# Idle columns on TensorE around and inside the products of decay and V, in a cross-attention and expert kernel

## The chip, the cores and the metric

The kernel runs on one core of one Trainium2 chip. The metric is the device time of the kernel in microseconds (us), as the median of its runs. Beside it stands one profiled execution, with the span from its first to its last instruction, the times of each engine, and the clock that TensorE was granted.

The engines are called by their short names: PE (TensorE, matrix products; PEld is its weight load), DVE (VectorE), ACT (ScalarE), POOL (GpSimd) and SP (which issues DMAs).

## The reference

Two layers, each added to its input x, of 32 batches of 128 tokens with 256 features:

```python
# attention of the mLSTM kind: q = layernorm(x), k = v = ctx, 8 heads of 32 features
cs = cumsum(log_sigmoid(fg))
log_D = cs_s - cs_t + ig_t            # masked to t <= s
D = exp(log_D - max_t log_D)
C = (q k^T / sqrt(32)) * D
h = C / (max(|sum_t C|, exp(-max_log_D)) + 1e-6) @ v
x = x + groupnorm(h) * out_w
# mixture of 8 experts, two for each token
x = x + sum_k gate_k * (gelu(xn @ w1[e_k] + b1[e_k]) @ w2[e_k] + b2[e_k])
```

## The kernel before

The work has two parts. The first runs over eight steps of four batches each (SB = 4, j = 0 to 3): normalise x, turn x and ctx, gates, decay matrix, scores, the product with V, normalise h, add to x, route the tokens and scatter them to a table sorted by expert. The second part runs the experts over tiles of up to 256 rows from that table, and adds the results to the output.

In the first part each engine runs a list of helpers in an order that is written out by hand, and semaphores tie the engines together. One pass of `body(last, step, nxt, after)` holds pieces of four steps: the routing of `last`, the end of the attention of `step`, the decay matrix and first scores of `nxt`, and the turning and gates of `after`. So one period of the loop holds the work of one whole step, spread over four.

The names that matter for the change, on PE:

- `decay_args` (L942, L946, L949) builds the exponents of the decay matrix of one batch and half of its heads in one PSUM bank, `turn_bank`; ACT takes the exp of it (L706). Its last product is the identity times `never`, 512 columns in bf16.
- `scores(j)` (L997) makes the 24 products of q and k of one batch, in f16 halves of 32 rows. DVE multiplies the scores by the decay matrix (`c_of`, L1355) and counts up `s_cm`. The scores of the next batch wait for that count, since there is one place for scores.
- `times_v(j)` (L1011) makes 16 products of 128 rows and 33 columns in f32, eight heads by two: the weights are the 128x128 blocks of the product of scores and decay, and the columns are V with a column of ones. All go to the first 264 columns of one bank, `ps_h` (named `pv` in the profile). It waits for `s_vc` (V ready), `s_cm`, and `s_hev`: ACT's eviction of that bank for the batch before it (`h_out`, L726 and L727).
- `turn_a` (L977) turns a column of gates, on which the running maximum and the split of it (`running_max`, L1304, and `split`, L1322) wait on DVE. `turn_max` (L983) turns the running maximum.
- `gates` (L963), `log_f_sum` (L971), `turn`, `q_left`, `turn_xf`, `xf_left`, `logits` and `ranks` are the other work of PE in a period.

On DVE a period is a fixed list: the four `c_of`, `next_stats` and `next_norm`, `weights_low` (expert weights split into halves), `running_max` and `split`, `h_norm` (which waits for the last eviction of times-V, L1365), `h_scaled` (which waits for ACT's guess of the root, L638), `choose`, `x1_of`, `x1_stats` and `records`.

Batches 0 and 1 of a step's times-V run at the end of one pass and batches 2 and 3 at the start of the next. After the eighth step the same helpers are written out once more, with the first expert tiles laid between them.

Of the kernel before, what the change touches and what calls it, by code (L numbers as in the profile page):

```python
# [13 lines left out]
P = 128  # L14
# [32 lines left out]
def build(nc, x, ctx_in, igate_w, igate_b, fgate_w, fgate_b, out_w, gate_w, w1, b1, w2, b2, out):  # L47
# [5 lines left out]
    NE, _, F = w1.shape  # L53
    FC = F // P
    SB = 4
# [41 lines left out]
    with ExitStack() as ctx:  # L97
        def sb(name, shape, dt=F32):
            return ctx.enter_context(nc.sbuf_tensor(name, shape, dt))

        def sem(name):
            return ctx.enter_context(nc.semaphore(name))
# [24 lines left out]
        ident_h = sb("ident_bf16", [P, P], BF16)  # L127
        minus_h = sb("minus_ident_f16", [P, P], F16)
        never = sb("minus_big_above", [P, P], BF16)
# [97 lines left out]
        ps_h = ctx.enter_context(nc.psum_tensor("pv", [P, 512], F32))  # L227
# [77 lines left out]
        s_hev = sem("h_in_sbuf")  # L305
# [23 lines left out]
        def number(step):  # L329
            return step[0] * 2 + step[1]  # L330

        def some(step, n):

            return not (isinstance(step[0], int) and number(step) < n)
# [72 lines left out]
        with nc.Block() as block:  # L407
# [494 lines left out]
            def _(pe):  # L902
# [31 lines left out]
                def decay_args(step, j, r):  # L934

                    g = number(step)
                    if j == 0 and r == 0:
                        pe.wait_ge(s_sp, g * 2 + 2)
                    if j + r or some(step, 1):
                        pe.wait_ge(s_ee, g * (2 * SB) + (2 * j + r))  # L940
                    first = j * NH + r * HG
                    pe.matmul(ps_t[:, :], parts[:, step[1], 0, :],  # L942
                              pick[:, first:first + HG].unsqueeze(2).broadcast_to([3 * G, HG, P]),
                              start=True, stop=False)
                    for u in range(HG):
                        pe.matmul(ps_t[:, u * P:(u + 1) * P],  # L946
                                  unpick[:, first + u:first + u + 1].broadcast_to([3 * G, P]),
                                  parts[:, step[1], 1, :], start=False, stop=False)
                    pe.matmul(ps_t[:, :], ident_h[:, :], never[:, :].unsqueeze(1).broadcast_to([P, HG, P]),  # L949
                              start=False, stop=True).then_inc(s_ar, 1)  # L950
# [23 lines left out]
                def turn_a(step):  # L974
                    g = number(step)
                    pe.wait_ge(s_a, g + 1)
                    pe.transpose(ps_aT, acol[:, :, :].rearrange("p r g -> p (r g)"), ident[:, :]).then_inc(s_aT, 1)  # L977

                def turn_max(step):
                    g = number(step)  # L980
                    pe.wait_ge(s_run, g + 1)
                    pe.sem_inc(s_held, 1)
                    pe.transpose(ps_ab, runs[2 * G:, 1, :], ident[2 * G:3 * G, 2 * G:3 * G]).then_inc(s_ab, 1)  # L983

                def scores(step, j):

                    g = number(step)
                    if j == 0:
                        turned = 1 if isinstance(g, int) and g == NSTEP - 1 else 2
                        pe.wait_ge(s_ql, g * SB + turned * SB)  # L990
                    if j or some(step, 1):
                        pe.wait_ge(s_cm, g * SB + j)
                    for u in range(KC):
                        for n, (a, b) in enumerate(HALVES):
                            for k in range(HG):
                                r = slice(DH * k, DH * k + DH)
                                ins = pe.matmul(ps_s[:, k, u * P:(u + 1) * P], qkT[r, step[1], j, a, KC + u, :],  # L997
                                                qkT[r, step[1], j, b, u, :], start=(n == 0), stop=(n == 2))
                    ins.then_inc(s_s, 1)

                def times_v(step, j):
                    g = number(step)
                    if j == 0:
                        pe.wait_ge(s_vc, g + 1)
                    pe.wait_ge(s_cm, g * SB + j + 1)
                    if j or some(step, 1):
                        pe.wait_ge(s_hev, g * SB + j)
                    for u in range(KC):
                        for k in range(HG):
                            h = u * HG + k  # L1010
                            ins = pe.matmul(ps_h[:, h * (DH + 1):(h + 1) * (DH + 1)], E[:, j, k * KC + u, :],  # L1011
                                            vaug[:, step[1], j, h, :], start=True, stop=True)
                    ins.then_inc(s_pv, 1)

                def turn_xf(step, r):
                    g = number(step)
                    pe.wait_ge(s_xf, g * SB + 2 * r + 2)
                    if r:
                        pe.wait_ge(s_xl, g * (SB // 2) + r)
                    elif some(step, 1):  # L1020
                        pe.wait_ge(s_rec, g)
                    else:
                        pe.wait_ge(s_cd, 1)
                    for j in range(2):
                        for c in range(KC):
                            ins = pe.matmul(ps_x[:, (j * KC + c) * P:(j * KC + c + 1) * P],
                                            xfn[:, step[1], 2 * r + j, c * P:(c + 1) * P], ident[:, :],
                                            is_transpose=True, start=(j == 0 and c == 0), stop=(j == 1 and c == KC - 1))
                    ins.then_inc(s_xt, 1)
# [32 lines left out]
                def body(last, step, nxt, after):  # L1062
                    if step is not None:
                        scores(step, 3)
                        times_v(step, 2)
                    if nxt is not None:
                        turn_a(nxt)
                    if last is not None:
                        turn_xf(last, 0)
                    if step is not None:  # L1070
                        times_v(step, 3)
                    if nxt is not None:
                        decay_args(nxt, 0, 0)
                    if after is not None:
                        turn(after, 0)
                    if last is not None:
                        xf_left(last, 0)
                    if after is not None:
                        turn(after, 1)
                    if nxt is not None:  # L1080
                        decay_args(nxt, 0, 1)
                    if last is not None:
                        turn_xf(last, 1)
                    if after is not None:
                        q_left(after, 0)
                    if nxt is not None:
                        decay_args(nxt, 1, 0)
                    if last is not None:
                        xf_left(last, 1)
                    if after is not None:  # L1090
                        turn(after, 2)
                        q_left(after, 1)
                    if last is not None:
                        logits(last)
                    if after is not None:
                        turn(after, 3)
                    if nxt is not None:
                        decay_args(nxt, 1, 1)
                    if after is not None:
                        q_left(after, 2)  # L1100
                    if nxt is not None:
                        turn_max(nxt)
                    if after is not None:
                        q_left(after, 3)
                    if nxt is not None:
                        decay_args(nxt, 2, 0)
                        scores(nxt, 0)
                    if after is not None:
                        gates(after)
                    if nxt is not None:  # L1110
                        decay_args(nxt, 2, 1)
                        scores(nxt, 1)
                        times_v(nxt, 0)
                    if last is not None:
                        ranks(last)
                    if nxt is not None:
                        decay_args(nxt, 3, 0)
                        scores(nxt, 2)
                        times_v(nxt, 1)
                    if after is not None:  # L1120
                        log_f_sum(after)
                    if nxt is not None:
                        decay_args(nxt, 3, 1)
# [651 lines left out]
```

## Time and profile before

| | |
|---|---|
| median of 3 runs | 737.8 us (736.86 to 738.75) |
| the profiled execution, its own time | 738.3 us |
| its span | 736.5 us |
| mean granted clock of TensorE over the span | 0.884 |
| PE busy | 671.3 us (91%) |
| DVE busy | 529.6 us (72%) |
| ACT busy | 316.8 us (43%) |
| POOL busy | 196.2 us (27%) |

The granted clock is given as a share of full speed: 1.00 is 2.4 GHz and 0.50 is 1.2 GHz, and a value between them is the mean over a stretch with both. A wait in the profile is idle time of an engine, named after the instruction that ended it. Products on PE are pipelined, so the time from the start of one group to the start of the next is what a group costs, not its length in the row.

### The profile page before, as it was taken

What the parts mean: (1) busy time and instruction counts of PE and PEld (TensorE: products, weight loads), DVE (VectorE), ACT (ScalarE), POOL (GpSimd) and SP (SyncE); (2) the same over time, 40 slices, a digit from 0 to 9 for tenths busy, and PEclk for the clock granted to TensorE, in tenths of its full rate; (3) what the DMA queues carried; (4) which work ended last, traced back from release to release, by engine and by line L of the source; (5) the groups of instructions that cost most, each with busy time, mean ns of one, the idle gap of its engine ahead of it and who ended that gap; (6) DMA issues with size and microseconds to landing.
All of it is one profiled execution on the core that took longest, in us unless ns stands there. A gap on an engine that the chain in (4) does not pass through costs nothing. (4 is left out here: it accounts for less than half of the span.)

```text
span 736.5 us, 19825 instructions
## 1 busy us (share of the span) xinstructions
PE 671.3 (91%) x6379; PEld 568.2 (77%) x6380; DVE 529.6 (72%) x1434; ACT 316.8 (43%) x743; POOL 196.2 (27%) x178
## 2 busy tenths in 40 slices
PE   2397999898999899989999999999999999999994
PEld 1265868585868567878998998888988898898873
DVE  3659888989798958498778867657766666766652
ACT  4377575766575733345423323323323323323321
POOL 2000004140404032225335413313323322322334
PEclk9998785858575955699999999999999999999998
DMA  3534353645445121614336423223223223323000
GB/s 126 171 116 136 123 170 101 210 132 171 146 145 174 63 87 60 207 40 105 56 69 201 84 53 62 40 52 59 41 42 58 40 48 59 49 39 60 7 4 2
DMA packets 56037, 66.45 MB, mean 90 GB/s; under 512 B 6480, under 2 KB 51728, under 8 KB 55840
## 3 DMA queue, kind: packets, MB, share of 16 engines
q1 hardware_dynamic: 41552, 48.13, 21.3%
q0 software_dynamic: 14304, 17.32, 12.9%
q8 instruction: 43, 0.70, 0.4%
q14 instruction: 26, 0.21, 0.1%
q10 hardware_dynamic: 112, 0.08, 0.1%
HBM read 41.50 MB, written 25.84 MB: 91 GB/s over the span
## 5 line engine op out<-in xcount | busy, mean ns | idle before, releaser
L838 ACT ACTIVATE decay_slots<-scores,b_turned 128x256 f32<-128x256 f32 (+1 forms) x312 | 126.2, 460 | 260.5 <-PE scores L1145 259.5
L1145 PE MATMUL scores<-x_slots,w_halves 128*128 128x256 f16 (+1 forms) x1872 | 207.5, 269 | 0.8 <-issue 0.8
L1145 PEld LDWEIGHTS scores<-x_slots,w_halves 128*128 x1872 | 177.8, 98 | 23.1 <-issue 1.4
L585 POOL DMA_INDIRECT expert_rows<-xf_rows,slot_i x64 | 68.0, 1063 | 281.6 <-issue 126.7
L1159 PE MATMUL pv<-w_halves,decay_slots 128*128 x912 | 103.0, 273 | 0.0
L1011 PE MATMUL pv<-v_centred_and_one,decay_slots 128*128 128x33 f32 x512 | 99.8, 365 | 2.0 <-issue 1.2
L1011 PEld LDWEIGHTS pv<-v_centred_and_one,decay_slots 128*128 128x128 f32 x512 | 96.2, 289 | 6.8 <-issue 3.9
L1159 PE MATMUL gate_bank<-w_halves,q_and_k_halves 128*128 x864 | 97.5, 273 | 0.0
L1159 PEld LDWEIGHTS pv<-w_halves,decay_slots 128*128 128x128 f16 x912 | 88.9, 98 | 10.9 <-issue 0.3
L604 POOL DMA_INDIRECT out_rows<-v_centred_and_one,row_ids x40 | 63.2, 1580 | 127.0 <-DVE v_centred_and_one L1686 105.6
L604 POOL DMA_INDIRECT out_rows<-work,row_ids x38 | 59.8, 1573 | 128.0 <-DVE work L1686 110.2
L1159 PEld LDWEIGHTS gate_bank<-w_halves,q_and_k_halves 128*128 128x128 f16 x864 | 84.3, 98 | 10.1
L1673 DVE TENSOR_TENSOR decay_slots<-decay_slots 128x512 f16<-128x512 f32 (+1 forms) x80 | 53.3, 667 | 2.7
L706 ACT ACTIVATE decay_slots<-turn_bank 128x512 f32<-128x512 f32 x64 | 38.4, 599 | 37.2 <-PE turn_bank L949 37.1
L1673 DVE TENSOR_TENSOR q_and_k_halves<-decay_slots,q_and_k_halves 128x512 f16<-128x512 f32 (+1 forms) x76 | 50.5, 665 | 2.6
L1355 DVE SCALAR_TENSOR_TENSOR decay_slots<-scores,decay_slots 128x1024 f32<-128x1024 f32 x32 | 39.1, 1223 | 6.8 <-PE scores L997 5.9
L1662 DVE CAST x_slots<-turn_bank 128x512 f16<-128x512 f32 (+1 forms) x39 | 25.9, 664 | 20.5 <-PE scores L1145 13.4
L1346 DVE SCALAR_TENSOR_TENSOR w_halves<-weight_stage,w_halves 128x1024 f16<-128x1024 f32 x32 | 39.0, 1221 | 1.9 <-ACT w_halves L718 1.7
L718 ACT ACTIVATE w_halves<-weight_stage 128x1024 f16<-128x1024 f32 x32 | 33.7, 1054 | 10.5 <-DMA weight_stage<-in_L_ffn_w 10.2
L942 PE MATMUL turn_bank<-pick_head,three_parts 96*128 96x512 bf16 x64 | 31.5, 492 | 5.3 <-DVE three_parts L1322 3.1
L1671 DVE CAST decay_slots<-decay_slots 128x512 f16<-128x512 f32 (+1 forms) x80 | 34.3, 429 | 2.7 <-ACT decay_slots L838 2.6
L946 PEld LDWEIGHTS turn_bank<-three_parts,minus_pick_head 96*128 96x128 bf16 x256 | 25.1, 119 | 13.1 <-issue 8.5
(244 smaller groups left out, 810.3 us busy)
## 6 DMA issues: line engine op xcount, KB each, us to landing
weight_stage<-in_L_ffn_w SPq DMA_DIRECT2D x32, 512.0 KB, 4.2
x_slots<-in_x SPq DMA_DIRECT2D x16, 512.0 KB, 4.0
weight_stage<-expert_rows SPq DMA_DIRECT2D x30, 272.0 KB, 3.1
ctx_slots<-in_ctx SPq DMA_DIRECT2D x8, 512.0 KB, 4.8
out_rows<-x_slots SPq DMA_DIRECT2D x8, 512.0 KB, 4.0
v_centred_and_one<-expert_rows SPq DMA_DIRECT2D x9, 272.0 KB, 3.4
expert_rows<-v_centred_and_one SPq DMA_DIRECT2D x9, 272.0 KB
expert_rows<-xf_rows,slot_i POOLq DMA_INDIRECT x64, 2.6
```

The lines of the kernel that those rows point to most:

```text
L585: pool.indirect_dma_start(table, bass.IndirectOffsetOnAxis(ap=sloti[:, step[1], j, k:k + 1], axis=0), xfn[:, step[1], j, :], None, bounds_ ...
L604: pool.indirect_dma_start(out_rows, bass.IndirectOffsetOnAxis(ap=ids[:, k, b:b + 1], axis=0), yo[k][:, b, :], None, bounds_check=T - 1, oo ...
L706: act.activation(E[:, j, HG * r:HG * r + HG, :].rearrange("p c s -> p (c s)"), ps_t[:, :], ACT.Exp).then_inc(s_ee, 1)
L718: act.activation(dst, stage[:, half, :], ACT.Copy, scale=W_SCALE).then_inc(s_hi, 1)
L838: ins = act.activation(hf[:, f * R:f * R + tr.rows(0)], ps_s[:, q, n * R:n * R + tr.rows(0)], ACT.Gelu, bias=b1T[:, bass.ds(expert, 1), f] ...
L1011: ins = pe.matmul(ps_h[:, h * (DH + 1):(h + 1) * (DH + 1)], E[:, j, k * KC + u, :], vaug[:, step[1], j, h, :], start=True, stop=True)
L1145: ins = pe.matmul(o, w, xh[:, tr.slot(0) % 2, b, k, 0:tr.rows(0)], start=(n == 0), stop=(n == 3 * KC - 1))
L1159: ins = pe.matmul(ps_y[k % 2][:, c * D:(c + 1) * D], hh[k % 2][:, a, f, c * P:(c + 1) * P], w, start=(f == 0 and n == 0 and c == 0), stop= ...
L1346: dve.scalar_tensor_tensor(out=lo, in0=stage[:, half, :], scalar=W_SCALE, in1=hi, op0=ALU.mult, op1=ALU.subtract).then_inc(s_lo, 1)
L1355: dve.scalar_tensor_tensor(out=c, in0=ps_s[:, :, 0:KC * P], scalar=QK_SCALE, in1=c, op0=ALU.mult, op1=ALU.mult).then_inc(s_cm, 1)
L1671: dve.tensor_copy(hi, src).then_inc(s_hhi, 1)
L1673: dve.tensor_tensor(lo, src, hi, ALU.subtract).then_inc(s_hh, 1)
```

## The change

PE gets products whose results nobody reads. They multiply the bf16 identity by the constant matrix `never` and write to the bank of times-V, `ps_h`. `stream(n)` issues n of them, 512 columns each, over the whole bank. Three stand ahead of every `times_v(j)`, behind the wait for the eviction and ahead of the waits for V and for the decayed scores. Inside `times_v`, ahead of every second product (eight heads in two halves, so four times a group as it is written: k = 0 and 2 of each u, for two values of u), one of 240 columns goes to the columns 272 to 512 of the bank, which the results do not use. `stream_between` issues two at three further places of a step: ahead of `turn_max`, ahead of `scores(0)` and ahead of `scores(1)`; in the first step it issues none.

```diff
+                def stream(n):
+
+                    for _ in range(n):
+                        pe.matmul(ps_h[:, :], ident_h[:, :], never[:, :].unsqueeze(1).broadcast_to([P, SB, P]),
+                                  start=True, stop=True)
+
+                def stream_between(step):
+                    g = number(step)
+                    if some(step, 1):
+                        pe.wait_ge(s_hev, g * SB)
+                        stream(2)
+
                 def times_v(step, j):
                     g = number(step)
+                    if j or some(step, 1):
+                        pe.wait_ge(s_hev, g * SB + j)
+                    stream(3)
                     if j == 0:
                         pe.wait_ge(s_vc, g + 1)
                     pe.wait_ge(s_cm, g * SB + j + 1)
-                    if j or some(step, 1):
-                        pe.wait_ge(s_hev, g * SB + j)
                     for u in range(KC):
                         for k in range(HG):
                             h = u * HG + k
+                            if k % 2 == 0:
+                                pe.matmul(ps_h[:, P + P + 16:512], ident_h[:, :],
+                                          never[:, 0:120].unsqueeze(1).broadcast_to([P, 2, 120]), start=True, stop=True)
                             ins = pe.matmul(ps_h[:, h * (DH + 1):(h + 1) * (DH + 1)], E[:, j, k * KC + u, :],
                                             vaug[:, step[1], j, h, :], start=True, stop=True)
                     ins.then_inc(s_pv, 1)
...
                     if nxt is not None:
+                        stream_between(nxt)
                         turn_max(nxt)
                     if after is not None:
                         q_left(after, 3)
                     if nxt is not None:
                         decay_args(nxt, 2, 0)
+                        stream_between(nxt)
                         scores(nxt, 0)
                     if after is not None:
                         gates(after)
                     if nxt is not None:
                         decay_args(nxt, 2, 1)
+                        stream_between(nxt)
                         scores(nxt, 1)
                         times_v(nxt, 0)
```

## Rows read from the trace of the kernel before

**Rows 1.** The page: granted clock in 40 slices, and the weight loads of times-V

```profile
PEclk9998785858575955699999999999999999999998
...
L1011 PEld LDWEIGHTS pv<-v_centred_and_one,decay_slots 128*128 128x128 f32 x512 | 96.2, 289 | 6.8 <-issue 3.9
```

**Rows 2.** Busy time by stretches, one for each period of the loop

```profile
core 0: us, PE busy (x) PEld busy (x) DVE busy (x) ACT busy (x) POOL busy (x), PEclk, DMA share, GB/s
...
75.97:109.02 33.05, 30.22 (x322) 23.84 (x314) 27.78 (x76) 22.59 (x54) 0.00 (x0) 0.74 0.39 125
...
177.81:213.88 36.07, 33.40 (x330) 26.62 (x323) 30.26 (x89) 22.61 (x55) 9.11 (x8) 0.67 0.44 149
213.88:249.06 35.18, 33.55 (x331) 26.64 (x323) 30.01 (x89) 22.61 (x55) 8.56 (x8) 0.66 0.37 123
249.06:281.82 32.76, 28.79 (x262) 20.90 (x254) 24.44 (x73) 15.29 (x42) 8.12 (x8) 0.59 0.26 87
281.82:306.37 24.55, 24.55 (x165) 21.41 (x162) 14.46 (x61) 7.18 (x18) 7.75 (x8) 0.50 0.52 174
```

**Rows 3.** Waits of DVE, 109 to 249 us: total, times, longest

```profile
DVE a_and_running_max L1304 <- PE gate_bank L977: 5.1, 4, 1.8
DVE square_sum L1365 <- ACT work L727: 4.9, 4, 1.2
DVE h_newton L1221 <- ACT h_rstd L638: 2.0, 3, 0.8
```

**Rows 4.** Waits of DVE, 249.06 to 281.82 us

```profile
DVE a_and_running_max L1304 <- PE gate_bank L977: 2.6, 1, 2.6
DVE square_sum L1365 <- ACT work L727: 2.5, 1, 2.5
DVE h_newton L1221 <- ACT h_rstd L638: 1.8, 1, 1.8
```

**Rows 5.** Busy time by stretches around the changes of the granted clock

```profile
210.80:214.21 3.41, 2.91 (x89) 2.26 (x82) 3.37 (x7) 1.11 (x7) 0.00 (x0) 1.00 1.04 374
214.21:238.10 23.89, 23.89 (x160) 20.50 (x160) 20.09 (x64) 13.79 (x33) 8.56 (x8) 0.50 0.47 151
230.00:246.00 16.00, 14.87 (x122) 10.69 (x121) 13.06 (x34) 14.19 (x29) 3.52 (x3) 0.75 0.40 134
251.76:255.17 3.41, 2.02 (x38) 1.79 (x37) 3.13 (x18) 2.74 (x8) 0.00 (x0) 1.00 0.41 143
255.17:306.37 51.20, 48.63 (x350) 38.15 (x350) 33.21 (x110) 18.35 (x46) 15.86 (x16) 0.50 0.37 123
268.82:281.82 13.00, 10.97 (x109) 5.91 (x108) 10.43 (x32) 5.81 (x16) 0.20 (x1) 0.50 0.11 38
```

**Rows 6.** PE in order of time, first step: start, length, instruction, tile, count

```profile
50.74 0.38 PE L942 MATMUL turn_bank<-pick_head,three_parts 96*128 96x512 bf16 x1
50.96 0.39 PE L946 MATMUL turn_bank<-three_parts,minus_pick_head 96*128 96x128 bf16 x4
...
51.50 0.51 PE L997 MATMUL scores<-q_and_k_halves 32*128 32x128 f16 x24
51.94 1.97 PE L1011 MATMUL pv<-v_centred_and_one,decay_slots 128*128 128x33 f32 x16
53.75 0.39 PE L971 MATMUL gate_bank<-log_sigmoid,tri 128*128 128x32 f32 x2
```

**Rows 7.** PE in order of time, in the fifth step

```profile
188.50 0.63 PE L946 MATMUL turn_bank<-three_parts,minus_pick_head 96*128 96x128 bf16 x4
188.93 0.64 PE L949 MATMUL turn_bank<-minus_big_above,ident_bf 128*128 128x512 bf16 x1
189.50 0.83 PE L997 MATMUL scores<-q_and_k_halves 32*128 32x128 f16 x24
190.26 3.62 PE L1011 MATMUL pv<-v_centred_and_one,decay_slots 128*128 128x33 f32 x16
193.69 0.43 PE L977 MATMUL gate_bank<-ident,i_minus_sum 128*96 128x128 f32 x1
```

**Rows 8.** Waits of DVE, 48.93 to 75.97 us

```profile
DVE decay_slots L1355 <- PE scores L997: 1.4, 1, 1.4
```

## The prediction

> **What bounds the kernel now.** I read the clock line of the page first: the granted TensorE clock is full over the last three fifths of the run and well below it in the slices between about 50 and 300 us, which is the loop over the eight steps [rows 1]. The run's second part, the expert tiles, is bound by PE at full clock and is not touched; whatever the first part gains or loses is carried to the end. So the question is what sets the pace of the steps.
>
> The table by periods (from the first product of times-V of one step to that of the next) answers it [rows 2]. The five full periods from 75.97 to 249.06 us take 33.05 to 36.07 us each; in the last of them DVE is busy for 30.01 us, and between its operations there are many gaps of a tenth or so that are no wait. Its real waits are listed over four periods: 5.1 us for turn_a (L977), 4.9 us for the last eviction of times-V (L727), 2.0 us for the guess of h (L638), 12 us together or 3.0 us a period [rows 3]. I take the same for the first of the five. DVE is therefore the limit at about 32 us a period, and PE adds 3. PE is busy 33.55 us of the last, but at a mean clock of 0.66: that is work that grew, not work that is there.
>
> The two last stretches are different. From 249.06 to 281.82 no further step is behind, DVE is busy for only 24.44 us and waits 6.9 us [rows 2, 4]. From 281.82 to 306.37 PE is busy throughout at half clock, DVE only 14.46: there PE alone sets the time [rows 2].
>
> **Where the clock falls.** It holds at 2.4 GHz until times-V begins and falls to 1.2 GHz at 214.21, after a stretch with 2.91 us of 3.41 busy, then stays there for 23.89 us in which PE is busy without a break. It falls again at 255.17 after 2.02 us of 3.41, and stays low for 51.20 us [rows 5]. PE was thus not idle before the first fall; what it did there was thin: a decay argument sends 1,536 columns in about 0.7 us, a group of times-V 16 x 33 in 1.81 us, since each of its products comes with an f32 weight load [rows 6]. The clock came back (238.10) once times-V was done and the transposes and decay arguments had run alone.
>
> **The change, part by part.** It removes nothing. A step gets, per the diff, 12 products of 512 columns in front of the four groups of times-V, 6 at three other places (none in the first step), and 16 of 240 columns inside the groups.
>
> Prices: 512 columns take 0.22 us at 2.4 GHz (50.74 to 50.96) [rows 6] and 0.43 at 1.2 (188.50 to 188.93) [rows 7]; 240 columns by proportion 0.10 and 0.20. A group of 16 products takes 1.81 us (51.94 to 53.75) at full clock and 3.43 (190.26 to 193.69) at half [rows 6, 7], that is 0.113 and 0.214 us a product. Inside a group the stream needs its own weights and the weights of the next product after them. No row shows a narrow f16 stream between f32 products. From below nothing: the next load runs entirely beside the stream. From above, stream and one more product's pace, 0.2 us warm and 0.4 cold. The weight load's mean of 289 ns is longer than the pace of a product, so loads overlap what runs before them [rows 1]; I take half of the 0.10 or 0.20 us of the stream, 0.05 warm and 0.11 cold, rounded to 0.25 and 0.45 a group. A group with all its streams: 0.65 + 1.81 + 0.25 = 2.7 us warm; 1.28 + 3.43 + 0.45 = 5.2 us cold, 1.75 more than a cold group now. The Trainium skill (TensorE: Matmul & The Clock Gate, "Part 3: Packing small matmuls") says that a weight load overlaps matmuls in flight only in another row group; by it a group would cost 0.8 us more warm and 1.6 cold, and the last step below about 4.6 us more. The 289 ns against a pace of 113 speak against taking that as it stands, and the row decides here.
>
> *Does it keep the clock up?* With the streams one group sends 528 + 1,536 + 960 columns in 2.7 us, and scores and a decay argument go before and after it. That is much closer to the stretches in which the clock held than to bare times-V, so I expect 2.4 GHz through the groups of the five full periods, once the dense stretch has raised it. The weak places are where PE now runs ahead and waits: behind group 2, for next_a, and behind group 3, for split. A fall there hits group 3 or the decay arguments behind it; I allow for it in about every second step, at 1 us each.
>
> *Five full periods.* A warm group with streams takes 2.7 us in place of 3.43, scores 0.44 for 0.76 and a decay argument about 0.7 for 1.4 [rows 6, 7]. Over groups 1 and 2, two scores and two decay arguments that makes turn_a some 3.5 us earlier: its 1.3 us of waiting go, and so do the 1.2 for the eviction. Of the guess (0.5) nothing is taken. Gain 2.5 us a period, 12.5 in all, less 2.5 for the falls above: 10. The three streams at other places cost 3 x 0.43 = 1.3 us of PE, ahead of turn_max and scores 0 and 1; they lie beside ACT's copies and exps and in front of waits for DVE (choose, x1_of, c_of). If that cover is gone they cost up to 0.9 us a period, as two of them stand ahead of scores 0. The wait for s_hev moves ahead of those for s_vc and s_cm; the evictions are over by then, and nothing new queues behind it.
>
> *First step.* At full clock already, and DVE waits 1.4 us there for scores [rows 8]. One group's streams, 0.9 us, stand ahead of those scores: +1, to be paid.
>
> *249.06 to 281.82.* Groups warm. Of 2.6 and 2.5 us of waiting about 3.6 go in sum, as DVE has fewer fillers and reaches turn_a and h_norm sooner than in a full period: -3.6.
>
> *281.82 to 306.37.* Without turns and gates the stretch ahead of the last step's times-V is thin: even at half clock PE was busy for only 10.97 of 13.00 us [rows 5], at full clock it needs about 8, while DVE's chain from h_norm over choose and x1_of to c_of 0 stays as long. The streams ahead of scores 1 run before that wait and not in it, so about 3 us stay empty and I expect the clock to fall, as it did at 255.17. Then the four groups of the last step run at 1.2 GHz with all streams, with PE on the path: 4 x 1.75 = +7.0.
>
> Sum: -10 + 1 - 3.6 + 7 = -5.6 us. The profiled execution took 738.3 us, 736.5 of them span, against a median of 737.8: 732.7 less 0.5, I say 732.
>
> **The rivals.**
> - *Warm to the end.* The streams carry the clock into the last step as well. For it: 3 x 1,024 columns are added just there. Against it: the empty stretch. Then instead of +7 the last stretch shrinks: the four groups take 10.8 us in place of 13.7, scores and decay arguments save some 1.5 more, less about 0.4 of new waits, -4 in all: 738 - 10 + 1 - 3.6 - 4 = 721.
> - *The fall comes ahead of group 0 or 1 of full steps too* (the one that ends on the other side). One such step runs its groups at 1.2 GHz with streams: 4 x 1.75 = 7 us on top of today's step, and the 2.5 gained are lost, 9.5 for each. It decides from the first step on: one brings 741.5, three bring 760, all five 780. For it: the clock fell at 214.21 in spite of 2.91 of 3.41 us busy, and which instruction a fall meets moves from step to step. Against it: the streams are added on both sides of this point. I expect no return inside times-V after such a fall, as there was none before [rows 5].
> - *Nothing comes of the earlier PE.* The waits of DVE are replaced by ACT, whose chain from the last eviction over the copies of q and k to scores 0 is busy for 14.19 of the 16 us from 230 to 246 [rows 5], or by the streams ahead of scores 0 at 0.9 us a period. Then the five periods give 3 to 4 us and not 10: about 738.
> - *The streams do not count for the clock at all.* Then every step has 7 us of streams in times-V and 2.6 beside it, some of it hidden: 738 + 7 x 7 = 787.
>
> **How the numbers follow.** Forecast 0.50, with an own range of 726 to 737 (streams inside a group free to double, falls behind group 2 in no step or in each). Warm to the end 0.12. Falls ahead of the groups in one to three steps 0.20. ACT in place of PE 0.12. Not counted 0.06. The measurement tells 0.3%, 2.2 us, from no change, so faster begins below 735.6 and slower above 740.0. Faster: 0.85 of the first, all of the second, a little of the fourth: 0.58. Slower: nearly all of the third and the fifth, a little of the first: 0.27. Same 0.15. The range goes from 717 to 752, leaving out the worst of the third case, the fifth, and a result that is better than all terms.
>
> **What would show it.** In the profile after: granted clock 1.00 in the groups of times-V of the steps between 80 and 240 us, a group of times-V at 2.7 us, its streams included; DVE waits for L977 and L727 near zero; periods near 32.6 us; a fall shortly before the last step's times-V and half clock until layer 1 begins; from then on the same trace, shifted. The prediction is wrong if the clock falls between scores 1 and group 1 of a full step, if a group with its streams takes over 3.3 us at full clock, or if the last step is warm.

## The result

The change makes the kernel faster: 713.0 us in the median (712.1 to 714.7, four runs) against 737.3 for the kernel before, a ratio of 0.968 (95% interval 0.965 to 0.970). I had said 732 with a range from 717 to 752. The direction was right; the size was not, and the time lies outside the range. Medians here and below count every run, while ratios leave out the runs that lie more than 1.5% above the fastest of their kernel: five of ten for the kernel with the products ahead alone, three of ten for the one without those between, none of the others.

The page of the changed kernel, span, busy time and clock, answers to [rows 1]:

```profile
span 711.8 us, 20333 instructions
...
PEclk9589999999999979999999999999999999999998
...
L1027 PEld LDWEIGHTS pv<-v_centred_and_one,decay_slots 128*128 128x128 f32 x512 | 65.1, 198 | 3.9 <-issue 0.8
```

The clock is now nearly full from the fourth slice on, but for one slice and the last, and the weight loads of times-V take 65 us in place of 96. The lower second and third slices lie ahead of the first step, where PE is busy for only 18 of 46 us, and cost nothing (46.25 us up to the first step against 46.64). To see where the 24.7 us of span went I cut both traces at the multiplication of scores by decay of batch 0 (`c_of`) of the first, second, seventh and last step, which a whole period of DVE's list lies between. The columns are those of [rows 2]. Before the change:

```profile
46.64:73.68 27.04, 23.15 (x285) 17.45 (x284) 24.13 (x53) 18.39 (x42) 0.00 (x0) 0.87 0.44 141
73.68:247.34 173.66, 161.28 (x1642) 127.79 (x1641) 149.02 (x428) 113.07 (x264) 35.33 (x32) 0.70 0.44 146
247.34:279.79 32.45, 28.82 (x274) 21.15 (x271) 24.09 (x73) 14.86 (x37) 8.12 (x8) 0.62 0.25 84
279.79:736.48 456.69, 439.03 (x4040) 389.08 (x4038) 311.55 (x819) 147.19 (x357) 147.93 (x103) 0.96 0.31 62
```

And after it:

```profile
46.25:73.47 27.22, 25.00 (x343) 18.06 (x342) 24.06 (x54) 18.11 (x42) 0.00 (x0) 1.00 0.47 155
73.47:230.19 156.72, 138.31 (x1788) 98.54 (x1785) 147.51 (x429) 111.93 (x264) 36.52 (x32) 0.99 0.48 159
230.19:258.39 28.20, 24.21 (x311) 16.76 (x307) 24.09 (x73) 15.92 (x43) 8.25 (x8) 1.00 0.29 97
258.39:711.77 453.38, 435.58 (x4064) 384.67 (x4064) 311.82 (x819) 145.99 (x351) 147.29 (x103) 0.98 0.30 62
```

| stretch | before | after | measured | forecast |
|---|---|---|---|---|
| up to the first c_of | 46.64 | 46.25 | -0.4 | 0 |
| first step | 27.04 | 27.22 | +0.2 | +1 |
| five full periods | 173.66 | 156.72 | -16.9 | -10 |
| the step without one behind it | 32.45 | 28.20 | -4.2 | -3.6 |
| from the last step's first c_of to the end | 456.69 | 453.38 | -3.3 | +7 |

Two of these rows carry nearly all the error: 6.9 us in the full periods and 10.3 us in the last step.

In the five full periods PE does more (1,788 records against 1,642) in less busy time (138.3 against 161.3 us). DVE's busy time is nearly the same, 147.5 and 149.0 us. What went is its idle time. Its waits there, before (the three long ones of seven) and then after, answer to [rows 3]:

```profile
DVE a_and_running_max L1304 <- PE gate_bank L977: 6.4, 5, 1.8
DVE square_sum L1365 <- ACT work L727: 6.2, 5, 1.2
DVE h_newton L1221 <- ACT h_rstd L638: 2.8, 4, 0.8
...
```

```profile
DVE decay_slots L1374 <- PE scores L997: 0.6, 1, 0.6
DVE decay_slots L1374 <- issue: 0.3, 1, 0.3
DVE mean_var_x L1250 <- DVE bn_parts_x L1246: 0.2, 1, 0.2
```

The three waits, 15.4 us together, are gone, the one for ACT's guess of the root too; four short ones (1.6 us in all before) have become the three above. PE is what waits now, in the same stretch:

```profile
PE gate_bank L963 <- DVE max_log_d L1352: 4.2, 5, 0.9
PE turn_bank L942 <- DVE three_parts L1341: 3.4, 4, 1.0
PE turn_bank L942 <- ACT decay_slots L706: 2.6, 5, 0.5
PE scores L997 <- DVE decay_slots L1374: 2.4, 4, 0.9
...
```

Now the last step, PE in order of time (start, length, instruction, tile, count):

```profile
256.22 0.59 PE L1004 MATMUL pv<-minus_big_above,ident_bf 128*128 128x512 bf16 x2
259.67 0.83 PE L997 MATMUL scores<-q_and_k_halves 32*128 32x128 f16 x24 [2.85 <-DVE decay_slots L1374]
260.43 1.46 PE L1004 MATMUL pv<-minus_big_above,ident_bf 128*128 128x512 bf16 x3
...
265.57 0.59 PE L942 MATMUL turn_bank<-pick_head,three_parts 96*128 96x512 bf16 x1
265.95 0.63 PE L946 MATMUL turn_bank<-three_parts,minus_pick_head 96*128 96x128 bf16 x4
266.37 0.63 PE L949 MATMUL turn_bank<-minus_big_above,ident_bf 128*128 128x512 bf16 x1
266.94 0.83 PE L997 MATMUL scores<-q_and_k_halves 32*128 32x128 f16 x24
267.70 1.46 PE L1004 MATMUL pv<-minus_big_above,ident_bf 128*128 128x512 bf16 x3
268.95 0.41 PE L1025 MATMUL pv<-minus_big_above,ident_bf 128*128 128x240 bf16 x1
269.15 0.64 PE L1027 MATMUL pv<-v_centred_and_one,decay_slots 128*128 128x33 f32 x4
```

And the stretch at half clock:

```profile
259.11:269.35 10.24, 9.68 (x91) 6.85 (x91) 7.01 (x32) 2.16 (x6) 1.17 (x2) 0.50 0.16 53
```

The empty stretch of 2.85 us ahead of scores 1 is there as forecast (I had said about 3), and the clock falls at 259.11. But it is back at 269.35, in the first products of group 1, after a decay argument, scores and three idle products that PE ran one behind the other. The rest of group 1 and groups 2 and 3 run at 2.4 GHz.

There is one other fall in the steps, at 136.23 for 3.41 us. It stands not behind group 2 or 3, where I had looked for falls, but ahead of group 0 of a full step, the place of my second rival:

```profile
135.97 0.79 PE L1004 MATMUL pv<-minus_big_above,ident_bf 128*128 128x512 bf16 x2
136.69 0.83 PE L997 MATMUL scores<-q_and_k_halves 32*128 32x128 f16 x24
137.45 1.46 PE L1004 MATMUL pv<-minus_big_above,ident_bf 128*128 128x512 bf16 x3
```

The clock came back at 139.64, in the first products of group 0, and the period with this fall took 31.5 us like its neighbours.

One more thing that the rows say: a group of times-V has 16 records in the trace, but the new product of 240 columns stands ahead of every fourth of them. The group is eight products in two passes each, not 16 products as I wrote; the prices of a whole group are not touched by it. From its first idle product to the next instruction a group with all its streams takes 2.57 us at full clock and 4.90 at half (my prices: 2.7 and 5.2).

### The profile page after: what moved, and what is told of

It reads as the page before. It is cut to its first block and busy times, and to the rows that moved or that the text cites. A ratio compares the mean times of both kernels' runs of the same rounds, so it can differ in the third digit from the quotient of the medians.

```text
span 711.8 us, 20333 instructions
## 1 busy us (share of the span) xinstructions
PE 641.2 (90%) x6645; PEld 530.3 (75%) x6646; DVE 528.3 (74%) x1434; ACT 315.3 (44%) x743; POOL 196.9 (28%) x178
## 5 line engine op out<-in xcount | busy, mean ns | idle before, releaser
L1178 PEld LDWEIGHTS gate_bank<-w_halves,q_and_k_halves 128*128 128x128 f16 x864 | 84.4, 98 | 10.1
L1027 PEld LDWEIGHTS pv<-v_centred_and_one,decay_slots 128*128 128x128 f32 x512 | 65.1, 198 | 3.9 <-issue 0.8
L1027 PE MATMUL pv<-v_centred_and_one,decay_slots 128*128 128x33 f32 x512 | 65.2, 263 | 0.0
L1004 PE MATMUL pv<-minus_big_above,ident_bf 128*128 128x512 bf16 x138 | 40.8, 398 | 1.2 <-ACT work L727 1.0
L942 PE MATMUL turn_bank<-pick_head,three_parts 96*128 96x512 bf16 x64 | 25.5, 398 | 11.2 <-DVE three_parts L1341 5.9
```

What stands on the lines that cost most here:

```text
L1004: pe.matmul(ps_h[:, :], ident_h[:, :], never[:, :].unsqueeze(1).broadcast_to([P, SB, P]), start=True, stop=True)
L1178: ins = pe.matmul(ps_y[k % 2][:, c * D:(c + 1) * D], hh[k % 2][:, a, f, c * P:(c + 1) * P], w, start=(f == 0 and n == 0 and c == 0), stop= ...
```

## The experiments

Each kernel was timed beside the kernel before on the same chip. The ratios below are to that one; the change itself has 0.968 (0.965 to 0.970).

### One part alone, and one part taken away

The change has three parts: three idle products **ahead** of each group, four **inside** it, and two at each of three places **between**. All eight combinations were run. The edits take these lines from the changed kernel:

```diff
 # "ahead" out
-                    stream(3)
 # "inside" out
-                            if k % 2 == 0:
-                                pe.matmul(ps_h[:, P + P + 16:512], ident_h[:, :], ...
 # "between" out
-                    if some(step, 1):
-                        pe.wait_ge(s_hev, g * SB)
-                        stream(2)
+                    pass
```

Theory A was that the gain is nothing but the clock, and the question within it how wide the margin is. Theory B was that the moved wait matters.

> The change with all idle products taken out; only the wait for the eviction stands ahead of the waits for V and for the decayed scores. Theory A (the gain is the clock that the idle columns keep up): the same as before, 737 us, clock 0.88. Theory B (the moved wait takes part in it): clearly faster than before, by 3 us or more.

> Only the idle products of 240 columns inside times-V, none ahead and none at the three other places. Theory A with a thin margin (each part is needed): the clock still falls in most steps, as a group then sends some 1,500 columns and waits in front of it stay empty; 725 to 735 us. Theory A with a wide margin (any part does it): within 3 us of the full change, 713 to 716.

> Only the three idle products of 512 columns ahead of each group of times-V. They send 1,536 columns for each group against 960 from inside. Thin margin: falls in some steps, 715 to 725 us. Wide margin: 713 to 716.

> The full change without the two idle products at each of the three other places. If they are what carries the clock from the dense stretch into times-V, the clock falls ahead of group 0 in some steps and the time rises by about 3 us for each such step, to 716 or more. If the clock is held by what goes with times-V, the time is the same, 711 to 714, or 1 us less since 1.3 us of PE a period are gone.

> The full change without the idle products inside times-V; three ahead of each group and two at each of the three other places stay. A group of times-V at full clock is bare again (some 1.8 us with few columns). Thin margin: the clock falls in some steps inside or behind a group, 715 to 735 us with a wide spread between runs. If the inside ones are not needed once the others are there: 711 to 714.

> The full change without the three idle products ahead of each group; the inside ones and the three other places stay. Thin margin: as above, 715 to 735 us, since of a group's added 2,496 columns 1,536 are gone. Periods in which the clock falls inside times-V take 34 us, less than the 37.5 us of such periods with the streams ahead, as a group at half clock is 1.3 us shorter.

> Only the two idle products at each of the three other places; none ahead of the groups and none inside. Times-V is as thin as before the change, so the clock falls in it in each full step: 733 to 738 us, at most one stretch later than before.

| ahead | inside | between | median us (lowest to highest) | ratio (95%) | clock of the profiled execution |
|---|---|---|---|---|---|
| - | - | - | 737.8 (736.4 to 740.6) | 1.001 (0.999 to 1.003) | 0.877 |
| - | x | - | 734.1 (730.1 to 739.5) | 0.998 (0.994 to 1.001) | 0.888 |
| x | - | - | 742.3 (730.9 to 758.3) | 0.996 (0.992 to 1.000) | 0.907 |
| - | - | x | 732.0 (730.4 to 733.3) | 0.993 (0.991 to 0.996) | 0.894 |
| x | x | - | 734.0 (723.7 to 740.7) | 0.991 (0.987 to 0.995) | 0.922 |
| - | x | x | 730.1 (730.0 to 731.6) | 0.991 (0.988 to 0.994) | 0.900 |
| x | - | x | 725.7 (723.2 to 730.8) | 0.987 (0.982 to 0.993) | 0.934 |
| x | x | x | 713.0 (712.1 to 714.7) | 0.968 (0.965 to 0.970) | 0.970 |

For ahead alone median and ratio disagree: by the median of its ten runs it is 4.5 us slower than the kernel before (737.8), by the ratio it gains 0.4%. It is no gain to count on.

Theory B falls: the wait alone does nothing. Theory A stands with a thin margin. The three single parts give 0.2, 0.4 and 0.7% by the ratios, of which only the last is clear of noise, 1.3% in sum, and the three together 3.2%. Every combination that lacks a part still loses the clock for long stretches. So the parts are no three gains that add. The scatter goes with the products ahead where another part is missing: the runs of such kernels spread over 27 us (ahead alone), 17 (without between) and 8 (without inside), against 9 with inside alone, under 3 with between alone and under 2 without ahead (four to ten runs each).

My expectations of the first four were right for the wait and for inside alone. For ahead alone (715 to 725) and without between (3 us for each step in which the clock falls) they were too kind. Of the other three, without inside and without ahead came out as expected, and between alone (733 to 738) was 1 us faster than that. Without between, the clock holds through times-V for three periods and then falls ahead of group 0 in each of three steps; one of the three, then the first of the fallen ones and the next:

```profile
136.42:167.94 31.52, 27.27 (x354) 19.71 (x352) 29.80 (x90) 22.53 (x53) 8.87 (x8) 0.93 0.50 162
167.94:205.41 37.47, 34.77 (x357) 24.80 (x354) 30.19 (x90) 22.45 (x53) 9.54 (x8) 0.73 0.46 151
205.41:242.91 37.50, 34.80 (x357) 24.83 (x354) 30.30 (x90) 22.34 (x53) 9.66 (x8) 0.73 0.36 122
```

The same work takes 31.5 us with 3.4 us at half clock in the period and 37.5 with 20.5 us. That is my rival with the other sign, in a neighbour of the change: a period costs 6.0 us more than the one before it, where I had worked out 9.5, and 1.4 to 2.3 us more than the two last full periods of the kernel before [rows 2]. My price took all four groups as cold; here groups 0 and 1 are, and the clock comes back in group 2 (at 187.3 in the first of these periods). In front of the fall stands this, in the same kernel:

```profile
165.27 0.51 PE L997 MATMUL scores<-q_and_k_halves 32*128 32x128 f16 x24
166.93 1.45 PE L963 MATMUL gate_bank<-gate_w_halves,q_and_k_halves 128*128 128x16 f16 x48 [1.15 <-DVE max_log_d L1350]
168.23 0.59 PE L942 MATMUL turn_bank<-pick_head,three_parts 96*128 96x512 bf16 x1
```

The clock falls at 166.86. Ahead of it stands the wait of 1.15 us; the 48 products of 16 columns start only behind it. Of the three pairs of between, those ahead of `turn_max` and of `scores(0)` stand in front of this place in the full change, and the third behind it. In the full change PE waits there too (0.95 us, up to 134.09), and the fall at 136.23 behind it lasted 3.4 us and not 20.5.

Without ahead, the periods with a long fall mostly take 34.1 to 34.3 us, as expected: there a group at half clock is shorter by the three products (3.62 us against 4.90), and a fall costs less.

### The last step without its idle products

```diff
-                    stream(3)
+                    if not (isinstance(g, int) and g == NSTEP - 1):
+                        stream(3)
...
-                            if k % 2 == 0:
+                            if k % 2 == 0 and not (isinstance(g, int) and g == NSTEP - 1):
```

> The full change, but the last step's four groups of times-V have no idle products ahead or inside. My prediction of the last step said that its streams only cost 7 us there, since the clock does not return inside times-V; by that this version is about 5 us faster than the full change, 708. The trace after shows the clock back at 269.35, in group 1, with 10 us at half clock; if the streams bring that return, this version stays at half clock up to layer 1 and is 2 to 6 us slower, 715 to 719.

Measured: 715.5 us (714.7 to 716.4), ratio 0.972 (0.968 to 0.975), which still touches the interval of the change. The clock fell at 261.96 and stayed at half for 20.5 us, through groups 1 to 3. What came from my prediction (5 us faster) is not so; that the streams have a part in the return fits. But the stretch from the last step's first c_of to layer 1 of the first tile is hardly longer than in the full change. That stretch in the full change, and then in this kernel:

```profile
258.39:280.19 21.80, 19.50 (x197) 15.11 (x198) 13.49 (x56) 6.19 (x16) 6.69 (x7) 0.77 0.37 118
```

```profile
258.73:280.42 21.69, 20.41 (x169) 17.86 (x170) 13.96 (x56) 6.80 (x18) 7.75 (x8) 0.57 0.46 138
```

In this kernel PE waits for nothing between scores 1 and layer 1: with bare groups at half clock, PE alone sets the 21.7 us. The 12 first products of layer 1 then still run at half clock in part; from their start to that of the next 12 it takes 2.7 us, in the full change 1.75.

Is it the decay argument, scores and three idle products in a row that bring the clock back? Not by themselves. In the profiled execution of the kernel without inside the clock fell at 265.51, in group 0 of the last step, and the same row stood ahead of group 1:

```profile
268.48 0.83 PE L997 MATMUL scores<-q_and_k_halves 32*128 32x128 f16 x24
269.24 1.46 PE L1004 MATMUL pv<-minus_big_above,ident_bf 128*128 128x512 bf16 x3
270.49 3.46 PE L1024 MATMUL pv<-v_centred_and_one,decay_slots 128*128 128x33 f32 x16
```

There the clock stayed at half for 27.3 us, into layer 1. Lined up, with one profiled execution each, a fall ahead of or in group 0 of the last step lasted 10.2 us in the full change, without between and with ahead alone, 3.4 us with eight products inside and with six ahead, but 20.5 us with bare groups, 23.9 without ahead and 27.3 without inside. So no kernel without the products ahead that lost the clock in this step got it back before layer 1, and of those with them one did not either.

### The empty stretch of the last step filled

```diff
                         stream_between(nxt)
+                        if isinstance(number(nxt), int) and number(nxt) == NSTEP - 1:
+                            stream(12)
                         scores(nxt, 1)
```

> The full change and, in the last step alone, twelve more idle products ahead of scores 1, 2.6 us long at full clock, where the trace after has PE empty for 2.85 us before the clock falls at 259.11. If that empty stretch is what lets the clock fall, groups 0 to 3 of the last step run at full clock, and layer 1 of the first tile starts some 4 us earlier; the gathered rows of the first tile are then waited for, so 1.5 to 4 us faster than the full change, 709 to 711.5. If not: the clock falls all the same and the time is 713.

Measured: 714.6 us (714.0 to 719.3), ratio 0.974 (0.968 to 0.979): no faster than the change. The mechanism is confirmed: the clock no longer falls there, and groups 0 to 2 run at 2.4 GHz (it falls at 274.34 for 3.4 us). The last step is 0.8 us shorter, where I had expected layer 1 some 4 us earlier, because the rows gathered for the first expert tile come no sooner; and the profiled execution loses as much again, 0.7 us in the step before and 1.1 behind the first products of layer 1. The waits of PE in the last step and the first tile (255 to 300 us) of this kernel:

```profile
PE turn_bank L1151 <- DMA weight_stage<-expert_rows: 3.0, 1, 3.0
PE route_bank L1062 <- DVE chosen L1461: 2.4, 1, 2.4
PE turn_bank L1151 <- issue: 1.2, 1, 1.2
PE scores L997 <- DVE decay_slots L1376: 0.3, 1, 0.3
```

In the full change the first of these is 1.0 us. So the last step takes 21.0 us with full clock up to group 3 (258.52 to 279.55), 21.8 with the fall and the return, and 21.7 with three cold groups that have no idle products. In the kernel without inside, with the idle products ahead in place, group 0 mostly at full clock and groups 1 to 3 cold, it took 26.1 (262.13 to 288.21), against 23.35 before the change (279.79 to 303.14). From the last c_of to the end that kernel took 459.85 us, 3.2 more than before the change. This is nearly the case that I had priced, less the products inside. By my prices it is 3 x 1.28 for the products ahead of groups 1 to 3, less what full clock saved on group 0 (3.0 us against 3.4) and on the scores ahead of it (0.3): 3.1. The price of cold groups holds.

### And the idle places of the first tile

```diff
+                def ranks_after(s):
+                    pe.wait_ge(s_hev, NSTEP * SB)
+                    stream(6)
+                    ranks(s)
+                    stream(6)
-                tile_turn(Turn(0, 0), ..., (logits, sixth), (ranks, sixth)))
+                tile_turn(Turn(0, 0), ..., (logits, sixth), (ranks_after, sixth)))
```

> As the one before, and six idle products each ahead of and behind ranks in the first expert tile, where PE waits 1.4 and 1.4 us in the trace after and the clock falls for 3.4 us at 289.83. If the clock stays up there, layer 1 of the second tile saves 1.2 us: 0.5 to 1.5 us faster than the one before.

Measured: 714.3 us (713.1 to 717.2), ratio 0.972 (0.967 to 0.976), within the noise of the one before and of the change. I had expected 0.5 to 1.5 us less than that one. The fall at the ranks is gone, but the clock fell at 275.22, in the wait for the gathered rows, for 6.8 us, where the one before had 3.4. No version beat the change.

### More columns inside a group

```diff
-                            if k % 2 == 0:
+                            if True:
                                 pe.matmul(ps_h[:, P + P + 16:512], ...
```

> The full change with an idle product of 240 columns ahead of each of the eight products of a group, eight and not four. The trace after has a group at 1.69 us from its first to its last product, as before the change, so four streams inside cost nothing. If a stream hides beside the weight load of the product behind it, eight do too: 1.7 us a group, and 711 to 714 us. If half of each load's time was free and is now used up, a group takes 0.2 us more or so and the time stays within 1 us, as DVE sets the period; if a stream costs its 0.1 us, the group takes 2.1 to 2.5 us.

Measured: 714.5 us (713.9 to 715.5), ratio 0.970 (0.967 to 0.974). A group with eight idle products takes 1.82 us from its first to its last record, with four 1.69, with none 1.70 in the kernel before; the start of one with eight:

```profile
234.59 0.27 PE L1025 MATMUL pv<-minus_big_above,ident_bf 128*128 128x240 bf16 x1
234.69 0.32 PE L1027 MATMUL pv<-v_centred_and_one,decay_slots 128*128 128x33 f32 x2
234.84 0.27 PE L1025 MATMUL pv<-minus_big_above,ident_bf 128*128 128x240 bf16 x1
```

The 1.70 is not the right thing to compare with, and I had concluded too soon that four cost nothing. With three idle products ahead and none inside a group takes 1.59. The bare groups of the kernel before show the same without any idle product: at half clock they take 3.22 us behind scores, but 3.06 in group 3 of the last step, where a product of 512 columns (L931) stands ahead of them. So some 0.1 us is saved by what stands ahead. From the first idle product to the next instruction it is 2.36 us with none inside, 2.57 with four and 2.69 with eight: four cost 0.21 us and eight 0.33, for 0.4 and 0.8 us of columns. The nearest of my three cases is the middle one.

### Twice as much ahead

```diff
-                    stream(3)
+                    stream(6)
```

> The full change with six idle products of 512 columns ahead of each group of times-V in place of three: 0.65 us more of PE for each group at full clock, 2.6 us a period, 21 us over the eight steps. If DVE sets the period now (it is busy for 29.8 of 31.6 us, and PE waits some 3 us a period), nearly all of it is hidden: periods of 31.5 to 32.5 us, in all 712 to 717. If PE is still on the path, 725 to 734.

Measured: 719.6 us (716.8 to 724.5), ratio 0.978 (0.972 to 0.985). The five full periods of it:

```profile
75.62:234.50 158.88, 148.93 (x1864) 102.57 (x1861) 147.89 (x429) 111.75 (x264) 35.12 (x32) 1.00 0.48 158
```

PE is busy for 10.6 us more than in the full change and the periods take 2.2 us more: DVE sets their pace (147.9 us busy, in the full change 147.5), and PE has had room. The first step has none; it took 29.3 us (46.32 to 75.62) against 27.2, with DVE waiting 5.0 us for scores. The step without one behind it took 1.7 us more and what follows 2.2 more, 8.2 in all. I expected 712 to 717 and had forgotten the steps outside the full periods.

## Why the prediction was wrong

**Right.** The reading of what bounds the steps (DVE, with some 3 us of waits a period that PE adds), the place of the fall in the last step and its cause (with the empty stretch filled it did not come), and the price of a group: 0.65 ahead, which the records show as 0.66, and 0.25 inside against 0.21; at half clock 1.28 ahead against 1.25, and 0.45 inside against 0.37. The three single parts were not weighed in the prediction, but its second rival's counterweight ("the streams are added on both sides of this point") proved to be needed: without those between, the point gives way.

**The step that failed: the last step, "with all streams, with PE on the path: +7.0".** It measured -3.3, an error of 10.3 us. What failed is "I expect no return inside times-V after such a fall, as there was none before": it took the bare groups of before as evidence for groups with idle products. The fall came where I said, but only group 0 ran cold to its end, and not four groups. The clock was back after 10.2 us, in group 1, and it also came back inside times-V in each of the three long falls in the steps of the kernel without between. The cost of a cold group is not what failed: where groups 1 to 3 did stay cold with the products ahead, the stretch was longer by 2.7 us where my prices give 3.1.

Of the -3.3, 1.6 lies in the last step (21.80 us against 23.35) and 1.6 in layer 1, whose first products run at full clock now (1.75 us from the start of the first 12 to that of the next 12, 3.33 before); I had written "from then on the same trace, shifted". PE is on the path in this step when its groups are cold, even bare ones (21.7 us). When they are not, it waits for the gathered rows, and the step takes 21.0. So little more was to be won there.

**The term that was mis-sized: the five full periods, -10 against -16.9.** Of the 6.9 us, 2.5 is the allowance for falls behind groups 2 and 3. None came there in the profiled execution; the one fall that came stood ahead of group 0, lasted 3.4 us and cost nothing. Some 2.8 us is the guess of the root, of which "nothing is taken": that wait disappeared. ACT's waits for times-V in this stretch went from 31.4 to 10.1 us, so that it may have reached the guess sooner, but no run tests that. The rest, 1.6 us, is in the main DVE's own work, which took 1.5 us less (149.0 to 147.5) and which I had left as it was; no run tells why. The first step, +1 against +0.2, was not "at full clock already": its mean clock was 0.87 before and is 1.00 now.

**The rivals.** "Warm to the end" said 721 and was the nearest case, but it was not what happened: the clock did fall where I said. That its -4 for the last step is near the measured -3.3 is luck, since half of that came from layer 1. "The fall comes ahead of group 0 of full steps too" did happen, once: the clock was low from scores 1 into group 0, which comes close to one of my signs of being wrong. But it was back after 3.4 us, and nothing of the 9.5 us was paid: an early return again, as in the last step. "ACT in place of PE" did not come: DVE waits for ACT nowhere in the five periods now. "Not counted" is refuted by the full change. My range ended at 717 because the one large positive term was taken as certain in all cases but one, with 0.12.

**What stays open.** What brings the clock back inside times-V is not settled. The idle products have a part in it, by the executions lined up above, but with one profiled execution of each kernel the place at which a fall meets the program is not held fixed, and without between the same groups that returned after 10.2 us in the last step needed 20.5 in three full steps. Why a wide product ahead of a group shortens it by 0.11 us, no run tells. Why ahead alone scatters over 27 us and the full change over 3 was only argued: the falls depend on where they meet the program, and a fall costs more with the products ahead in place (periods of 37.5 us against 34.1).

## What to carry to other kernels

If a matrix engine is busy and yet has lost its clock, look for what it does that has few columns: here f32 products of 33 columns with a full weight load each. Idle columns can then be worth more than they cost, but test them all together: here no part alone gave more than 0.7% and three gave 3.2%, and leaving one out cost some 60 to 70% of that. Price the gain on the engine that sets the pace (here DVE's 15 us of waits, not PE's 23 us of shorter work), and before pricing a cold stretch at the end, ask what else is late there.

## What the runs showed of the hardware

- A product of 240 columns in bf16 ahead of or between f32 products with 128x128 weights costs less than its columns: eight in a group added 0.33 us, where their columns alone are 0.8 us, and four added 0.21. The Trainium skill (TensorE: Matmul & The Clock Gate, "Part 3: Packing small matmuls"), by which a weight load does not run beside a product that uses the same rows, would have made that about 0.2 us each by my estimate in the prediction; the rows disagree. That section excepts loads into a background weight buffer, and no run here tells whether these were such loads.
- A group of times-V takes 1.69 us from its first to its last record at full clock and 3.23 at half. A period of the kernel without between takes 31.5 us with 3.4 us of it at half clock, and 37.5 with 20.5.
- A wide product straight ahead of such a group shortens it: 1.59 us against 1.70 at full clock, 3.06 against 3.22 at half.
- Products whose results are never read count for the granted clock: 0.877 without any and 0.970 with all of them, on the same work.
